# Two expert stages: first-layer weights through a transfer ring and into the stationary place, so that the middle tile comes out turned

## What is computed

```python
def _L0_ffn_ref(x, sg, su, sd, rg, ru, rd, wr, rb):      # H, I, E_ROUTED, TOP_K = 128, 352, 7, 2
    def _expert(h, g, u, d):
        return jnp.einsum('...i,hi->...h', jax.nn.silu(h @ g.T) * (h @ u.T), d)
    shared_out = _expert(x, sg, su, sd)
    scores, idx = jax.lax.top_k(softmax(x @ wr.T + rb), TOP_K)
    ...
    for e in range(E_ROUTED):
        out = out + w[..., e:e + 1] * _expert(x, rg[e], ru[e], rd[e])

def _L1_ffn_ref(x, w_gate, b_gate, W1, b1, W2, b2):      # D_MODEL, MLP_DIM, N_EXPERTS = 128, 512, 8
    h = jax.nn.relu(jnp.einsum('nd,edm->enm', x_flat, W1) + b1[:, None, :])
    y = jnp.einsum('enm,emd->end', h, W2) + b2[:, None, :]
    out = y[route_idx, jnp.arange(n)] * route_p[:, None]
```

## Time and profile before

| | us |
|---|---|
| median of 3 runs | 1050.17 |
| lowest, highest | 1045.48, 1050.59 |
| the profiled execution, its own time | 1048.49 |
| its span, first to last instruction | 1046.7 |
| stage a, first T to last scatter's issue | 625.5 to 729.8 |
| stage b, first T to last scatter's issue | 967.1 to 1034.0 |

### The profile page before, as it was taken

One profiled execution on the slowest core, in us unless ns is written; L12 is line 12 of the kernel. 1 busy time (PEld: TensorE's weight loads), 2 busy tenths in 40 slices (PEclk: granted clock), 3 DMA queues, 4 the chain that ended last, 5 costly groups with the idle time before them and its releaser, 6 DMA issues. The chain is left out here.

```text
span 1046.7 us, 19177 instructions
## 1 busy us (share of the span) xinstructions
PE 818.4 (78%) x6209; PEld 659.3 (63%) x6210; DVE 598.2 (57%) x1968; ACT 523.0 (50%) x1100; POOL 368.9 (35%) x510
## 2 busy tenths in 40 slices
PE   3789999999999999999876979997064645540993
PEld 3667878888788888888664656776053535340672
DVE  7546666675766666566754323332768687860333
ACT  1466667666676766676543414444154545430331
POOL 0153222322322332332212563455634343216342
PEclk9899999999999999999866999999567787755997
DMA  9990000000000000000001111111900000001113
GB/s 285 295 65 1 2 1 2 1 1 2 2 1 1 2 2 2 2 2 1 2 1 40 39 56 45 49 52 36 341 0 1 0 0 0 1 0 51 45 45 98
DMA packets 46294, 41.09 MB, mean 39 GB/s; under 512 B 11883, under 2 KB 40891, under 8 KB 45707
## 3 DMA queue, kind: packets, MB, share of 16 engines
q1 hardware_dynamic: 42731, 32.91, 13.0%
q0 software_dynamic: 3488, 7.20, 2.1%
HBM read 27.85 MB, written 12.30 MB: 38 GB/s over the span
## 5 line engine op out<-in xcount | busy, mean ns | idle before, releaser
L1700 POOL TENSOR_TENSOR sb_expd<-sb_expd,sb_rden 128x512 f32<-128x512 f32 (+1 forms) x128 | 112.5, 879 | 335.8 <-DVE sb_rden L1273 335.8
L1260 DVE TENSOR_REDUCE sb_smax<-bank 128x4 f32<-128x512 f32 (+1 forms) x128 | 73.9, 577 | 115.3 <-PE bank L515 115.0
L948 ACT ACTIVATE sb_probT<-bank 128x512 f32<-128x512 f32 (+1 forms) x128 | 75.6, 591 | 50.4 <-PE bank L528 50.3
L528 PE MATMUL bank<-sb_eye,sb_expd 128*128 128x128 f32 (+1 forms) x512 | 82.5, 286 | 11.8 <-POOL sb_expd L1700 11.5
L783 PE MATMUL bank<-sb_eye,sb_z_all 128*128 128x128 f32 x96 | 24.6, 423 | 81.2 <-ACT sb_z_all L1049 81.2
L489 PE MATMUL bank<-sb_h1T,sb_watt 128*128 128x128 f32 x512 | 72.2, 287 | 7.5 <-DMA sb_watt<-att_wo 7.5
L528 PEld LDWEIGHTS bank<-sb_eye,sb_expd 128*128 128x128 f32 (+1 forms) x512 | 59.8, 148 | 28.5 <-POOL sb_expd L1700 26.6
L1262 DVE TENSOR_TENSOR sb_shifted<-bank,sb_smax 128x512 f32<-128x512 f32 (+1 forms) x128 | 75.0, 586 | 4.4
L1269 DVE TENSOR_REDUCE sb_row_sum<-sb_expd 128x4 f32<-128x512 f32 (+1 forms) x128 | 73.2, 572 | 5.0 <-ACT sb_expd L953 4.9
L953 ACT ACTIVATE sb_expd<-sb_shifted 128x512 f32<-128x512 f32 (+1 forms) x128 | 69.3, 542 | 9.2 <-DVE sb_shifted L1262 8.9
L540 PE MATMUL bank<-sb_probT,sb_v 128*64 128x128 f32 (+1 forms) x1024 | 71.8, 283 | 2.7 <-issue 1.5
(11 more groups left out here) (251 smaller groups left out, 1979.3 us busy)
## 6 DMA issues: line engine op xcount, KB each, us to landing
sb_watt<-att_w SPq DMA_DIRECT2D x6, 512.0 KB, 5.7
sb_gate_up<-gate_up SPq DMA_DIRECT2D x1, 2816.0 KB, 13.1
sb_gate_up<-b SPq DMA_DIRECT2D x1, 2560.0 KB, 21.3
sb_blk_x<-rows_a SPq DMA_DIRECT2D x38, 65.0 KB, 1.8
rows_a<-sb_zeros SPq DMA_DIRECT2D x1, 2432.0 KB, 30.7
sb_picked<-back_a SPq DMA_DIRECT2D x4, 512.0 KB, 5.7
sb_w1b<-w1b SPq DMA_DIRECT2D x1, 2048.0 KB, 12.2
sb_down<-down SPq DMA_DIRECT2D x1, 1536.0 KB, 15.1
```

The source lines that it names most:

```text
L528: mm = pe.transpose(trans[u % 2][0:n, h, :], expd[:, u % 2, h, 0:n], eye[:, :])
L948: act.activation(probT[0:n, u % 2, :, :], trans[u % 2][0:n, :, :], ACT.Copy).then_inc(probT_ready, 1)
L1260: dve.tensor_reduce(smax[:, u % 2, :], s_in, X, ALU.max).then_inc(max_done, 1)
L1700: pool.tensor_tensor(e, e, rden[:, u % 2, :].unsqueeze(2).broadcast_to([P, QH, n]), ALU.mult).then_inc(norm_done, 1)
```

## The change

The first-layer weights of a block no longer lie in SBUF as a table. SP loads them for each block into a ring of four places, `up_w`, right behind the block's rows: 128 x 768 floats (384 KB, gate and linear half padded from 352 to 384 columns) in stage a, 128 x 512 (256 KB) in stage b. In the up product the weights are now the stationary operand, in pieces of 128 columns, and `blk_xT` is the moving one. So the middle tile comes out with its features on the partitions, as down needs it: the turns of the middle tile (L764, L867) and the copies of them (L1030, L1032, L1106) are gone, and down of block n stands in step n, one step earlier than before. In stage b ACT now adds the bias and applies Relu, from the bank to `blk_h`, in four instructions with a bias column each; DVE's sum is gone. DVE's order in stage a is turned: first the result of block n-1, then the product of block n+1. The loads of `w1b`, of all of `gate_up` but the shared expert, and of the first biases as rows are gone. Line numbers in the order's rows of the kernel after are its own.

```diff
-        gate_up = sb("gate_up", P, EA + 1, 2 * IA)
+        gate_up = sb("gate_up", P, 2 * CA * P)
...
+        up_w = sb("up_w", P, NSLOT, 2 * CA * P)
...
+            def load_weights(x, m, u):
+                table, n_exp, src, n = {"a": (expert_a, EA, A["gate_up"], 2 * CA * P), "b": (expert_b, EB, A["w1b"], FB)}[x]
+                e = sp.value_load(table[0:1, bass.ds(m, 1)], min_val=0, max_val=n_exp - 1)
+                from_one(sp, up_done[x], m - NSLOT + 1)
+                sp.dma_start(up_w[:, u, 0:n], src[bass.ds(e, 1), :, :].rearrange("a p n -> (a p) n")).then_inc(up_w_in[u], 16)
...
                     for u in range(NSLOT):
                         load(x, src, NSLOT * q + u, u)
+                        load_weights(x, NSLOT * q + u, u)
...
             def step_a(q, u):                                   # PE
...
                 turn_rows("a", q, u)
                 if exists(n + 1, NR):
+                    pe.wait_ge(up_w_in[(u + 1) % NSLOT], 16 * (q + 1 + (u + 1) // NSLOT))
                     for j in range(2):
-                        mm = pe.matmul(bank[1 + 2 * j + v][:, 0:IA], blk_xT[:, v, :],
-                                       gate_up[:, bass.ds(e_up, 1), j * IA:(j + 1) * IA].rearrange("p a n -> p (a n)"),
-                                       start=True, stop=True)
+                        for c in range(CA):
+                            mm = pe.matmul(bank[1 + 2 * j + v][:, c * P:(c + 1) * P],
+                                           up_w[:, (u + 1) % NSLOT, (j * CA + c) * P:(j * CA + c + 1) * P],
+                                           blk_xT[:, v, :], start=True, stop=True)
                     mm.then_inc(up_done["a"], 1)
                 if exists(n, NR):
                     pe.wait_ge(h_ready["a"], n + 1)
-                    from_one(pe, hT_ready["a"], n)
+                    from_one(pe, y_ready["a"], n - 1)
                     for c in range(CA):
-                        w = min(P, IA - c * P)
-                        mm = pe.transpose(bank[5][0:w, c * P:(c + 1) * P], blk_h[:, here, c * P:c * P + w], eye[:, :])
-                    mm.then_inc(hT_done["a"], 1)
...
+                        mm = pe.matmul(bank[6 + here][:, 0:D], blk_h[:, here, c * P:(c + 1) * P],
+                                       down[:, bass.ds(e_down, 1), c, :].rearrange("p a n -> p (a n)"),
...
             def step_b(q, u):                                   # ACT
                 turned_rows("b", q, u, NB)
...
+                if exists(n + 1, NB):
+                    e = act.value_load(expert_b[0:1, bass.ds(n + 1, 1)], min_val=0, max_val=EB - 1)
+                    act.wait_ge(up_done["b"], n + 2)
+                    from_one(act, y_done["b"], n)
+                    for c in range(FB // P):
+                        ins = act.activation(blk_h[:, v, c * P:(c + 1) * P], bank[1 + v][:, c * P:(c + 1) * P], ACT.Relu,
+                                             bias=b1_cols[:, bass.ds(e, 1), c:c + 1].rearrange("p a n -> p (a n)"))
+                    ins.then_inc(h_ready["b"], 1)
```

More of the change, by code:

```diff
@@ L362, in program @@
         NBLK = {"a": NR, "b": NB}
+        IN_BEFORE = {"a": [0] * NSLOT, "b": [len(range(u, NR, NSLOT)) for u in range(NSLOT)]}
         RANK_BANK = {"a": 7, "b": 2}
@@ L719, in _ @@
                     for j in range(2):
[L720 removed]
+                        mm = pe.matmul(bank[1 + CA * j + c][0:w, :], gate_up[:, (j * CA + c) * P:(j * CA + c) * P + w],
                                        flat(zsT, g), start=True, stop=True)
@@ L1025, in step_a @@
                     act.wait_ge(up_done["a"], n + 2)
[L1026 to L1033, removed]
+                    act.activation(blk_act[:, v, 0:CA * P], bank[1 + v][:, 0:CA * P], ACT.Silu).then_inc(act_done["a"], 1)
             skewed(act, NR, step_a)
@@ L1432, in step_a @@
             def step_a(q, u):
-                n, v, here = NSLOT * q + u, 1 - u % 2, u % 2
-                if exists(n + 1, NR):
-                    dve.wait_ge(act_done["a"], n + 2)
-                    dve.tensor_tensor(blk_h[:, v, 0:IA], bank[3 + v][:, 0:IA], blk_act[:, v, 0:IA],
-                                      ALU.mult).then_inc(h_ready["a"], 1)
+                n, v = NSLOT * q + u, 1 - u % 2
                 if exists(n - 1, NR):
@@ L1440, in step_a @@
                     leave("a", q, u, bank[6 + v], meta[:, bass.ds(n - 1, 1), 1:2].rearrange("p a n -> p (a n)"), ALU.mult)
+                if exists(n + 1, NR):
+                    dve.wait_ge(act_done["a"], n + 2)
+                    dve.tensor_tensor(blk_h[:, v, 0:CA * P], bank[3 + v][:, 0:CA * P], blk_act[:, v, 0:CA * P],
+                                      ALU.mult).then_inc(h_ready["a"], 1)
             def leave(x, q, u, t, other, op):
@@ L1653, in step_b @@
             def step_b(q, u):
-                n, v, here = NSLOT * q + u, 1 - u % 2, u % 2
-                if exists(n + 1, NB):
-                    dve.wait_ge(up_done["b"], n + 2)
-                    e = expert_of(n + 1)
-                    dve.tensor_tensor(blk_h[:, v, :], bank[1 + v][:, :], b1b[:, bass.ds(e, 1), :].rearrange("p a n -> p (a n)"),
-                                      ALU.add).then_inc(h_ready["b"], 1)
+                n, v = NSLOT * q + u, 1 - u % 2
                 if exists(n - 1, NB):
```

87 lines of the change are left out of this document (37 added, 50 removed).

## The result

The changed kernel takes 1024.23 us (median of 4 runs, 1019.71 to 1027.71) against 1049.89 for the kernel before in the same comparison: ratio 0.9755, 95% interval 0.9727 to 0.9784. Forecast were 1028.5 us and a range of 1018 to 1042. The profiled execution took 1022.9 us, 25.6 less than the one of before.

| part, us | before | after | difference | forecast |
|---|---|---|---|---|
| stage a: first T to last scatter's issue | 104.32 | 90.77 | -13.6 | -11.7 |
| between, to the first T of b | 237.3 | 237.4 | 0.1 | 0 |
| stage b: first T to last scatter's issue | 66.87 | 54.52 | -12.4 | -9.1 |

What follows compares the result with a forecast made beforehand. PE's array and sequencer were taken as close limits in stage a, and stage b alike. Stage a -11.7 and stage b -9.1 sum to -20.8 us; 1048.5 gives 1027.7, adjusted to 1028.5, range 1018 to 1042.

Steps and rivals of the forecast that it cites:

- rival (2): Both loops: PE's sequencer runs ahead and the branch hides; steps 2.14 and 2.0, POOL's 1.99 the floor, 1020.5 us; chance 0.14.
- The array's step of before, 2.41: Stage a before: PE's array alone needs 1.41 + 0.33 + 0.67 = 2.41 us a step; the missing 0.22 is its sequencer.
- T and up 1.41: Stage a before: PE's own work for T and the up product in one step, read as 657.76 to 659.17.
- Step of a after: 2.28 taken, 2.24 worked out: Loop of stage a after: array 2.14 and the branch's 0.4 in one step of four give 2.24; 2.28 us taken.
- The 0.04 that I added for late first passes: Loop of stage a: a late first pass would add up to 0.09 us a step, so 2.28 was taken over 2.24.
- Step of b: 2.25 taken: Loop of stage b after: chain 2.05 to 2.2 us plus 0.1 a step for the branch; 2.25 taken against 2.66.
- The next floor, 1.99: POOL's scatters at the kernel's end: 1.99 us a block, below the 2.28 step and 0.15 under the array.
- Starts and tails: Ends of both stages: start of a +1.8 us, its tail -2.3; start of b +1.3, its tail -3.0.
- SP 1.95 a block: SP's issues, waits and number load: 1.95 us a block, hidden by the 2.28 step; each 0.1 above costs 6 us.
- (1): Both loops: the wait ahead of the number's load makes the chain dearer, 2.45 a step, 1036.5 to 1040 us; chance 0.23.
- (3): Weight stream: ring loads don't overlap, steps 3.3 and 2.9 us, 1075 us in all, 1050 if half overlapped; chance 0.08.
- (4): Whole kernel: other limits, SP's pace at 2.6 or more low-clock steps, give the gain back; about 1049 us; chance 0.07.

Runs made afterwards that it cites:

- e3_extra: The changed kernel with each of PE's loads of an expert number done twice in a row; 1065.40 us, against 1047.25 for the changed kernel there.
- e2_late: The changed kernel with PE's expert-number load moved behind the up product, ahead of the middle-tile wait; 1042.45 us, against 1047.25 for the changed kernel there.

## Why the prediction held, and where it was off

The mechanism held in stage a: a sequencer above the array before, a chain as long as the array after, the branch uncovered, the stream hidden. In stage b the sum had PE's chain alone as the limit, and POOL was one as much. The measured 1024.23 lies inside the forecast's 1023 to 1033, but near its edge, and as near to the 1020.5 of rival (2) as to 1028.5; that it was the forecast's mechanism in a and not the rival's is told by the steps (2.46 to 2.49 at the branch), not by the time. The gain was 4.8 us more than the sum's -20.8, and these are the terms that were mis-sized.

- **The array's step of before, 2.41.** It was 2.29. What failed is "T and up 1.41", read from the start of T to the start of the turns: the same stretch takes 1.30 with the ring alone (690.45 to 691.75), so it held 0.11 in which the array waited for the sequencer. The turns and down in it were right, 0.33 and 0.67. This changes no term of the sum, which goes from measured step to worked-out step, but it made the split wrong: the sequencer was 0.32 a step, the turns saved on the array 0.17.
- **Step of a after: 2.28 taken, 2.24 worked out.** 2.21 came. Array 2.12 (2.14), the branch's step 2.46 to 2.49. The 0.04 that I added for late first passes isn't there. Over the loop and the unrolled steps together, from the start of up(2) to that of up(37), it makes 90.1 - 76.7 = 13.4 us instead of 11.2: half of what the sum missed.
- **Step of b: 2.25 taken.** 2.12 to 2.14 came. The four ACT instructions start 0.26 apart, the lower end; what ACT waits for ahead of them is the up product, so its own number load was covered. With the late load PE by itself is at 1.90 (1.92 worked out for the array), and what then held b was POOL's 2.11. "The next floor, 1.99" was read where POOL makes no copy for a coming block; in the loop it does, and needs 2.11. So the floor was already there in the stage where I had set PE's chain at 2.25. From up(3) to up(22), 976.02 to 1025.82 before and 963.18 to 1003.09 after, b won 9.9 us; 7.4 were forecast.
- **Starts and tails.** Start of a +1.75 (first T to up(2): 6.62, now 8.37), forecast +1.8. That this came so close is in part luck: PE waited last for the rows of block 1 (2.48 us, until 628.78), which the sum doesn't name, and up(0) at the low clock was no new cost, as it ran at that clock before too. Start of b +0.3 (first T to up(3), where the sum's steps begin: 8.89, now 9.16), forecast +1.3: I had carried over SP's 2 us a block, but at the start, with no waits and fixed addresses, its weights follow each other in 1.56 or 1.57. Tails -1.9 and -2.7 for -2.3 and -3.0.
- **SP 1.95 a block**, from pieces: 1.96 to 1.99 measured. There is less room in it than in the DMA engines: 0.44 us more a block cost 14 us, half more bytes nothing in the loop of a.

**The rivals.** (1), a chain dearer by 0.17, is refuted by the steps; e3_extra shows what a chain with a second number costs. (2), the hidden branch, came only by moving the load (e2_late): 3 of its 4 us in a, and none of those in b, where POOL stood in the way, at 2.11 and not at the 1.99 that the rival names. (3), a ring that doesn't overlap, is refuted twice over: the stream with loads of 384 KB ran at 238 GB/s, with 576 KB at 326. The rule of the Trainium skill (DMA: Bandwidth & Descriptors, "Bandwidth") on at least 1 MiB a transfer did not decide here: loads of a third of that, one behind the other, kept 0.84 of the engines' time busy and no product waited for its weights. The 81 ns a pass of the Trainium skill (TensorE: Matmul & The Clock Gate, "Back-to-back issue gap") did not come either; the up passes are 112 ns apart. (4) is refuted by the time; SP's pace of 2.6, its mechanism, was some 0.6 us a block away.

## What to carry to other kernels

Where an engine runs at 97% busy, take one register or number instruction from its sequencer, in a run that leaves the data path alone, before counting its array as the limit: here it told 0.32 us a step from 0.17. When a wait is moved, put what doesn't depend on it, number loads above all, in front of it and behind work that the array still has to do. When tables in SBUF become a stream, the issuing queue's instructions per block may be a nearer limit than the bytes: here half more bytes in the same loads cost nothing in the loop of a and 1.7 us in b, one small load more a block cost 14 us.

## What the runs showed of the hardware

- A second load of 2 KB per block cost some 14 us where 50% more bytes in one load cost nothing in the loop of a, at a DMA busy share of 0.97 and 326 GB/s: here that share near 1 was not yet a limit to what lands in time.
- With the stream beside them POOL's scatters of stage a take 3.9 us from issue to landing instead of 2.2 (medians). No wait of DVE or POOL for a free place of `blk_y` shows in the loop.
- A cast that POOL makes of the very destinations that its next scatter uses costs 0.21 us of idle time ahead of that scatter (0.82 against 0.61), on top of the cast's own 0.20.
- At the end of a stage, where POOL has no copy left to make for a coming block, its scatters lie 1.99 us apart; with the copy they lie 2.11 apart.
